# Eight token lists broadcast over the partitions by DMA, and a shorter chain to the quantised table, at the start of a fused language-model tower

## The reference

```python
def fake_quant(w):
    scale = max(abs(w)) / 127
    return round(w / scale) * scale
e = fake_quant(emb_weight)[x]                 # x: (8, 512) token numbers below 125
e = pad(e, one step ahead)                    # context of two tokens
h = relu(e[t-1] * w[0] + e[t] * w[1])         # w = fake_quant(conv_weight), per channel
h = h + attn(layernorm(h))                    # a linear recurrence over the 512 steps
h = h + ffn(layernorm(h))                     # 8 experts by position: 128 -> 512 -> 128, gelu
```

## Time and profile before

| | before |
|---|---|
| device time, median of 3 (lowest to highest) | 210.72 us (210.22 to 210.72) |
| span of the profiled execution (its own time outside the span is not on the page) | 206.2 us |
| TensorE busy | 181.0 us (88%) |
| VectorE busy | 143.2 us (69%) |
| ScalarE busy | 116.5 us (56%) |
| GpSimd busy | 97.5 us (47%) |
| moved by DMA | 7.60 MB |

### The profile page before, as it was taken

The page is one execution under the profiler, slowest core; times in us unless marked ns, Lnnn a source line. Parts: engine busy times, 40 slices in busy tenths (PEclk is TensorE's granted clock), DMA queues, the critical chain, the costliest instruction groups (busy, mean ns, idle before and its releaser), DMA issues. The chain is left out here.

```text
span 206.2 us, 4072 instructions
## 1 busy us (share of the span) xinstructions
PE 181.0 (88%) x1407; PEld 163.3 (79%) x1407; DVE 143.2 (69%) x411; ACT 116.5 (56%) x317; POOL 97.5 (47%) x144
## 2 busy tenths in 40 slices
PE   0498999999999999999694999988979979996993
PEld 0276789999899987887594898987969969995891
DVE  1859956753444434669587685995977959569994
ACT  2037986554433355454444577847759577693771
POOL 0116644999200002239576184672843917656441
PEclk9999999999999999999999699999999999999999
DMA  5991000000000000000000000010100100010012
GB/s 137 399 423 62 3 0 5 2 0 3 0 0 3 0 0 2 3 0 0 0 3 2 0 3 0 0 51 5 51 0 3 52 0 27 27 51 2 3 52 102
DMA packets 2566, 7.60 MB, mean 37 GB/s; under 512 B 309, under 2 KB 1122, under 8 KB 2290
## 3 DMA queue, kind: packets, MB, share of 16 engines
q1 hardware_dynamic: 2258, 7.15, 9.1%
q10 hardware_dynamic: 288, 0.20, 0.4%
HBM read 5.25 MB, written 2.10 MB: 36 GB/s over the span
## 5 line engine op out<-in xcount | busy, mean ns | idle before, releaser
L421 POOL TENSOR_TENSOR hid_p<-hid_f,hid_p 128x256 fp32r<-128x256 f32 x56 | 40.2, 734 | 35.8 <-ACT hid_p L566 27.6
L564 ACT ACTIVATE hid_f<-bank,pa 128x256 f32<-128x256 f32 x64 | 30.3, 478 | 22.6 <-PE bank L1091 22.6
L1091 PE MATMUL bank<-xaT_p,fc_p 128*128 128x256 f32 x192 | 35.7, 297 | 0.8 <-ACT hid_f L564 0.7
L1111 PE MATMUL bank<-hid_p,out_hi 128*128 128x256 f32 x128 | 33.6, 288 | 0.6 <-POOL hid_p L421 0.5
L473 ACT ACTIVATE X<-bank 128x128 f32<-128x128 f32 x64 | 17.6, 279 | 23.3 <-PE bank L935 23.1
L1091 PEld LDWEIGHTS bank<-xaT_p,fc_p 128*128 128x128 f32 x192 | 27.3, 191 | 3.4 <-issue 2.0
L932 PE MATMUL bank<-uT,pa 128*128 128x128 f32 x128 | 25.1, 280 | 0.1
L843 DVE TENSOR_SCALAR xp<-h,mv,rstd 128x128 f32<-128x128 f32 x32 | 22.5, 762 | 3.3 <-POOL rstd L439 3.3
L1111 PEld LDWEIGHTS bank<-hid_p,out_hi 128*128 128x128 f32 x128 | 23.8, 188 | 1.2 <-POOL hid_p L421 0.9
L935 PE MATMUL bank<-X,pa 128*128 128x128 f32 x120 | 23.2, 275 | 0.0
L566 ACT ACTIVATE hid_p<-bank,pa 128x256 fp32r<-128x256 f32 x48 | 23.0, 478 | 0.0
(11 more groups left out here) (123 smaller groups left out, 384.4 us busy)
## 6 DMA issues: line engine op xcount, KB each, us to landing
fc_w<-in_fc SPq DMA_DIRECT2D x2, 2048.0 KB, 11.2
out<-res SPq DMA_DIRECT2D x7, 256.0 KB, 2.0
pb<-in_pack_b SPq DMA_DIRECT2D x1, 320.0 KB, 4.2
pa<-in_pack_a SPq DMA_DIRECT2D x1, 279.0 KB, 3.5
out<-res SPq DMA_DIRECT2D x2, 128.0 KB, 1.7
conv_w<-in_conv ACTq DMA_DIRECT2D x1, 128.0 KB, 3.4
pc<-in_pack_c ACTq DMA_DIRECT2D x1, 66.5 KB, 3.8
rowsel<-in_rows SPq DMA_DIRECT2D x1, 64.0 KB, 3.8
```

Of the source, the lines that this page charges most:

```text
L421: nc.gpsimd.tensor_tensor(hid_p[1][:, half, c, :], hid_f[:, m % HID_SLOTS, :], hid_p[0][:, half, c, :].bitcast(F32), ALU.subtract).then_in ...
L564: full = nc.scalar.activation(hid_f[:, m % HID_SLOTS, :], src, ACT.Gelu, bias=bias)
L1091: last = mm(bank[5 + n % 2][:, 0:HALF], fc1_p[w][:, e * HID + c * P:e * HID + (c + 1) * P], xaT_p[m][:, b % 2, half, :], start=(k == 0), s ...
L1111: last = mm(out_bank(b, half)[:, half * HALF:(half + 1) * HALF], out_p[w][:, e, c * CH:(c + 1) * CH], hid_p[m][:, half, c, :], start=(c == ...
```

## The change

The 16 rows of ids, the cast, the selecting matrix and the spreading matmuls go. Each sequence's 544 ids are loaded as int32 onto 125 partitions, by one transfer that reads the same row 125 times: the first between `emb_w` and `pa`, the other seven after `pw` and ahead of `pb`. They count on three semaphores: batch 0, batches 1 to 3, batches 4 to 7. `one_hot(b)` is one instruction, reads SBUF, clips from above and compares; it is placed one round ahead of its gather where it was two.

The row maxima are transposed from a view that repeats them over 128 columns, so that the maximum is taken on all partitions at once. The rounding constant is added in the pass that scales and taken off in the passes that multiply by the taps; the bf16 product is computed anew in place of a cast. VectorE quantises the convolution weights before it reads the transposed maxima.

Gathers alternate between bank 2 and bank 0, and the first six `transpose_u` between bank 3 and bank 1. The waits of `gather`, `transpose_u` and the first `fuse_piece` follow from that. (Left out below: names of tensors and semaphores that only follow.)

```diff
 
             fc2_w = sb_early("fc2_w", [P, NE * HID])
             fc1_w = sb_early("fc1_w", [P, NE * HID])
-            ids_i = sb_early("ids_i", [2 * NB, EXT * NCH // 2], I32)
-            ids_b = sb_early("ids_b", [2 * NB, EXT * NCH // 2], BF16)
-            rowsel = sb_early("rowsel", [2 * NB, 2 * NB, P], BF16)
+            ids_i = sb_early("ids_i", [VOC, NB, EXT * NCH], I32)
...
@@ -320,6 +318,17 @@
         def scan_work(j, n):
             return plan[8 * (j + 3) + n]
 
+        IDS_GROUPS = (1, 3, 4)
+
+        def ids_group(b):
+            return 0 if b == 0 else 1 if b < 4 else 2
+
+        def gather_bank(b):
+            return bank[(2, 0)[b % 2]]
+
+        def u_t_bank(b):
+            return bank[1 if b % 2 == 1 and b < 6 else 3]
+
         P2_BANKS = ((4, 5, 0, 1), (6, 7))
 
         def fuse_bank(e):
@@ -351,10 +360,11 @@
             @block.sync
             def _(sp):
                 sp.dma_start(emb_w[:], emb).then_inc(ld_emb, 16)
-                sp.dma_start(ids_i[:], ids).then_inc(ld_ids, 16)
-                sp.dma_start(rowsel[:].rearrange("r j p -> r (j p)"), rows).then_inc(ld_ids, 16)
+                sp.dma_start(ids_i[:, 0, :], ids[0:1, :].broadcast_to([VOC, EXT * NCH])).then_inc(ld_ids[0], 16)
                 sp.dma_start(pa[:], pack_a).then_inc(ld_pa, 16)
                 sp.dma_start(pw[:, 1, :], pack_a[:, PA["a"]]).then_inc(ld_pa, 16)
+                for b in range(1, NB):
+                    sp.dma_start(ids_i[:, b, :], ids[b:b + 1, :].broadcast_to([VOC, EXT * NCH])).then_inc(ld_ids[ids_group(b)], 16)
                 sp.dma_start(pb[:], pack_b).then_inc(ld_pb, 16)
...
@@ -482,12 +492,12 @@
                         act.wait_ge(gat_done, b + 1)
                         if b == 0:
                             act.wait_ge(tab_ready, 1)
-                        nc.scalar.activation(h[:, b, :], bank[2][:], ACT.Relu, scale=scale_h[:]).then_inc(h_ready, 1)
+                        nc.scalar.activation(h[:, b, :], gather_bank(b)[:], ACT.Relu, scale=scale_h[:]).then_inc(h_ready, 1)
                     for t in prep_tasks(b, 0):
                         copy_out_prep(t)
                     if b >= 2:
                         act.wait_ge(u_t_done, b - 1)
-                        nc.scalar.activation(uT[:, b - 2, :, :].rearrange("p i k -> p (i k)"), bank[3][:],
+                        nc.scalar.activation(uT[:, b - 2, :, :].rearrange("p i k -> p (i k)"), u_t_bank(b - 2)[:],
...
@@ -612,38 +622,34 @@
                 dve.wait_ge(ld_conv, 16)
                 chained(nc.vector.tensor_reduce(scale_c[:], conv_w[:], AX.X, ALU.max, apply_absolute_value=True))
                 nc.vector.tensor_scalar(scale_c[:], scale_c[:], 1.0 / QMAX, None, ALU.mult).then_inc(scale_c_ready, 1)
-                dve.wait_ge(amax_t_done, 1)
-                nc.vector.tensor_reduce(amax_row[:], bank[6][0:1, 0:VOC], AX.X, ALU.max).then_inc(amax_row_ready, 1)
                 dve.wait_ge(scale_c_ready, 1)
                 chained(nc.vector.reciprocal(inv_c[:], scale_c[:]))
-                chained(nc.vector.tensor_scalar(q_c[:], conv_w[:], inv_c[:], None, ALU.mult))
-                nc.vector.tensor_scalar(q_c[:], q_c[:], ROUND, -ROUND, ALU.add, ALU.add).then_inc(q_c_ready, 1)
-
-                dve.wait_ge(ld_ids, 32)
-                nc.vector.tensor_scalar(ids_b[:], ids_i[:], -1.0, float(VOC - 1), ALU.max, ALU.min).then_inc(ids_ready, 1)
-                dve.wait_ge(amax_bc_done, 1)
-                chained(nc.vector.tensor_scalar(scale_e[:], bank[7][:, 0:1], 1.0 / QMAX, None, ALU.mult))
+                chained(nc.vector.tensor_scalar(q_c[:], conv_w[:], inv_c[:], ROUND, ALU.mult, ALU.add))
+                nc.vector.tensor_scalar(q_c[:], q_c[:], -ROUND, None, ALU.add).then_inc(q_c_ready, 1)
+
+                dve.wait_ge(amax_t_done, 1)
+                chained(nc.vector.tensor_reduce(amax_all[:], bank[6][:, 0:VOC], AX.X, ALU.max))
+                chained(nc.vector.tensor_scalar(scale_e[:], amax_all[:], 1.0 / QMAX, None, ALU.mult))
                 chained(nc.vector.reciprocal(inv_e[:], scale_e[:]))
-                chained(nc.vector.tensor_scalar(q_e[:], emb_w[:], inv_e[0:VOC, :], None, ALU.mult))
-                chained(nc.vector.tensor_scalar(q_e[:], q_e[:], ROUND, -ROUND, ALU.add, ALU.add))
+                chained(nc.vector.tensor_scalar(rounded[:], emb_w[:], inv_e[0:VOC, :], ROUND, ALU.mult, ALU.add))
                 dve.wait_ge(q_c_ready, 1)
 
-                for tap in range(2):
-                    last = nc.vector.tensor_tensor(prod[:, tap, :], q_e[:], q_c[0:VOC, tap * CH:(tap + 1) * CH], ALU.mult)
-                chained(last)
-                chained(nc.vector.tensor_copy(tab[:, 0], prod[:]))
+                both = rounded[:].unsqueeze(1).broadcast_to([VOC, 2, CH])
+                q_taps = q_c[0:VOC, :].rearrange("p (t c) -> p t c", t=2)
+                nc.vector.scalar_tensor_tensor(out=prod[:], in0=both, scalar=-ROUND, in1=q_taps,
+                                               op0=ALU.add, op1=ALU.mult)
+                chained(nc.vector.scalar_tensor_tensor(out=tab[:, 0], in0=both, scalar=-ROUND, in1=q_taps,
+                                                       op0=ALU.add, op1=ALU.mult))
                 nc.vector.tensor_tensor(scale_h[:], scale_e[:], scale_c[:], ALU.mult)
                 nc.vector.tensor_tensor(tab[:, 1], prod[:], tab[:, 0], ALU.subtract).then_inc(tab_ready, 1)
 
                 def one_hot(b):
-                    for s in range(2):
-                        n = 2 * b + s
-                        dve.wait_ge(idb_done, n + 1)
-                        if b >= 2:
-                            dve.wait_ge(gat_done, b - 1)
-                        w = EXT * NCH // 2
-                        nc.vector.tensor_scalar(onehot[:, b % 2, s * w:(s + 1) * w], bank[n % 2][0:VOC, 0:w],
-                                                pc[0:VOC, PC["iota"]], None, ALU.is_equal).then_inc(oh_ready, 1)
+                    group = ids_group(b)
+                    dve.wait_ge(ld_ids[group], 16 * IDS_GROUPS[group])
+                    if b >= 2:
+                        dve.wait_ge(gat_done, b - 1)
+                    nc.vector.tensor_scalar(onehot[:, b % 2, :], ids_i[:, b, :], float(VOC - 1),
+                                            pc[0:VOC, PC["iota"]], ALU.min, ALU.is_equal).then_inc(oh_ready, 1)
...
                 dve.wait_ge(ld_pc, 16)
                 one_hot(0)
-                one_hot(1)
                 for b in range(NB + 1):
-                    if b + 2 < NB:
-                        one_hot(b + 2)
+                    if b + 1 < NB:
+                        one_hot(b + 1)
...
@@ -875,7 +880,8 @@
                         if e == 0:
                             pe.wait_ge(ld_fc2, 16)
                             pe.wait_ge(ld_pb, 16)
-                            pe.wait_ge(oh_ready, 2 * NB)
+                            pe.wait_ge(h_ready, NB)
+                            pe.wait_ge(uT_ready, 6)
...
@@ -890,34 +896,28 @@
                     for c in range(HC):
                         fuse_piece(e, c)
 
-                def spread_ids(b):
-                    for s in range(2):
-                        n = 2 * b + s
-                        if n >= 2:
-                            pe.wait_ge(oh_ready, n - 1)
-                        mm(bank[n % 2][:, 0:EXT * NCH // 2], rowsel[:, n, :], ids_b[:], start=True,
-                           stop=True).then_inc(idb_done, 1)
-
                 def gather(b):
-                    pe.wait_ge(oh_ready, 2 * b + 2)
-                    if b >= 1:
-                        pe.wait_ge(h_ready, b)
+                    pe.wait_ge(oh_ready, b + 1)
+                    if b >= 2:
+                        pe.wait_ge(h_ready, b - 1)
                     for q in range(NQ):
                         for n, (tap, part) in enumerate([(0, 0), (0, 1), (1, 0), (1, 1)]):
 
                             at = (q * TQ + tap) * NCH
-                            last = mm(bank[2][:, q * CH:(q + 1) * CH], onehot[:, b % 2, at:at + P], tab[:, part, tap, :],
+                            last = mm(gather_bank(b)[:, q * CH:(q + 1) * CH], onehot[:, b % 2, at:at + P], tab[:, part, tap, :],
                                       start=(n == 0), stop=(n == 3))
                     last.then_inc(gat_done, 1)
 
                 def transpose_u(b):
                     pe.wait_ge(u_ready, b + 1)
                     pe.wait_ge(u_act_ready, sum(n < NQ for n in U_DVE[:b + 1]))
-                    if b >= 1:
+                    if b >= 6:
                         pe.wait_ge(uT_ready, b)
+                    elif b >= 2:
+                        pe.wait_ge(uT_ready, b - 1)
                     for q in range(NQ):
                         s = slice(q * CH, (q + 1) * CH)
-                        last = nc.tensor.transpose(bank[3][:, s], u[:, b % 2, s], ident)
+                        last = nc.tensor.transpose(u_t_bank(b)[:, s], u[:, b % 2, s], ident)
```

(35 more changed lines are left out.)

## The result

The changed kernel took 218.33 us in the median of 4 runs (216.77 to 218.62), the kernel before 210.47 beside it (208.18 to 210.72): a ratio of 1.042, 95% interval 1.036 to 1.048. (A kernel has a faster and a slower state on this chip; the ratio compares runs in the faster one alone and is not the quotient of the two medians, 1.037.) It is slower by 7.9 us by the medians and 8.9 by the ratio, where 2.2 were forecast, and the time lies outside the stated range, 211.0 to 214.5. The direction was as forecast, and so was its cause, loads on few engines. Two further losses on top of it, in the last ids loads and in TensorE's clock, were not in the sum.

What follows compares the result with a forecast made beforehand. The prediction took TensorE, full from 32 us on, as the bound, so delays entering that part move the end. Ids loads on five engines outweigh the earlier start: 210.7 + 2.2 = 212.9 us, range 211.0 to 214.5.

Steps and rivals of the forecast that it cites:

- Part 1, the chain: Start, chain to the quantised table: table at 7.91 us against 8.84, first gather at 8.5 instead of 10.05, 1.55 us earlier.
- Part 2: Rounds: the matmuls that spread the ids go, 0.3 to 0.4 us a round; VectorE saves 0.4 a round.
- Part 3: Second banks for gathers and `transpose_u`: help only when the next one-hot is there; the new fused-piece wait costs nothing.
- Part 4, five engines: Eight ids broadcast loads: 125 rows use five engines, 2.25 us each; TensorE's full part starts 2.2 us later; chance 0.70.
- The missing landing time: List of transfers: `emb_w`, the one load over 125 rows, has no landing time, taken as supporting five engines.
- Group 1: Ids loads of batches 1 to 3, sharing one semaphore: landing forecast at 14.2 us (13.3 to 15.0).
- Loads 4 to 7 follow: 14.2 + 9.0 = 23.2: Last ids group lands at 23.2 us, where `one_hot(4)` waits; gather 4 starts at 23.75 instead of 20.92.
- upper bound, 24.3: Latest landing forecast for ids loads 4 to 7, giving a delay of 3.3 us.
- the slow TensorE: Rival: after idling, gathers 2 to 5 and prep matmuls stay slow, up to 0.8 us a round; 214.5 us; chance 0.08.
- the likeliest case: Five engines carry each ids load, delaying TensorE's full part by 2.2 us: 212.9 us (211.2 to 214.0), chance 0.70.
- 4.5 us around the span: Time outside the 206.2 us span, up to the median of 210.72, taken as unchanged.
- hidden loads: Rival: sixteen engines share each ids load, 0.73 us each, no one-hot waits; 207.9 us; chance 0.12.

Runs made afterwards that it cites:

- E9: The changed kernel with ids loads over 128 rows, SP also waiting for `emb_w` before issuing anything else; 208.48 us, ratio 0.997 to the kernel before.
- E8: 128-row kernel, first ids load after `pa` and `pw`, three ids loads for eight, `pc` issued ahead of `conv_w`; 208.29 us, ratio 0.993 to the kernel before.
- E7: The kernel before with only the new chain to the table, ids still by matmuls; 209.07 us, ratio 0.998 to the kernel before.
- E12: E9 with batch 1's ids on a semaphore of their own (four groups: 1, 1, 2, 4); 205.94 us, ratio 0.985 to the kernel before.
- E1: The changed kernel with each ids load over 128 rows instead of 125; 207.88 us, ratio 0.995 to the kernel before.
- E2: The changed kernel, still 125 rows, SP issuing `pb`, `sel` and fc loads only after the last ids group landed; 211.66 us, ratio 1.014.
- E3: The changed kernel with 20 identity matmuls filling TensorE's idle stretch ahead of gather 4; 216.93 us, ratio 1.039 to the kernel before.
- E11: The changed kernel with 20 filling matmuls ahead of gather 4, on the same chip as E10; 215.93 us, ratio 1.033 to the kernel before.
- E4: E1 with all gathers in bank 2, transposes of `u` in bank 3 and the earlier waits; 207.50 us, ratio 0.994 to the kernel before.
- E6: The changed kernel with each ids load over 126 rows instead of 125; 208.25 us, ratio 0.995 to the kernel before.
- E10: The changed kernel once more, unaltered, on the chip of E11; 218.32 us, ratio 1.045 to the kernel before.

## Why the prediction was wrong

**Part 1, the chain: right in its own length, wrong in its start.** From the transpose to the start of the gather the prediction has 8.5 - 4.94 = 3.6 us. In the changed kernel that stretch is 7.15 to 10.58, 3.4 us; in E9, 4.27 to 8.44, 4.2, with the wait for `pw`. But the prediction left `pc` at 4.94. It landed at 6.4 to 7.8 in all nine profiles that have a load of 266 to 279 KB issued next to it; in E8, which has `pc` first, `conv_w` was late instead. In the four with small loads next to it, or none (before, E7, E9, E12), it was there at 4.2 to 5.2. The first gather started at 10.58. In the changed kernel this cost nothing, for `one_hot(1)` waited until 14.76 anyway; E12 takes it away from E1's kernel and splits the groups besides, and starts gather 7 at 29.16 instead of 30.97.

**Part 2: a little more than forecast, and covered. Part 3: nothing, as forecast.** The sum gave the matmuls that go 0.65 us between gather 4 and the full part. Where the clock stayed up (E2, E3, E11), gather 4 to gather 7 take 10.4 us instead of 11.2 before: 0.8. What of it is the matmuls' and what the shorter one-hot's, no run separates. In the changed kernel the fall of the clock covers it (12.05 us). For the second banks E4 shows that they bring nothing, in the kernel of 128 rows. The one-hot took 0.50 us in one pass, the value taken.

**Part 4, five engines: right.** 129 GB/s at a share of 0.33, and the 10 us between 125 and 128 rows, with 126 on the fast side, show it. The missing landing time, which the prediction read as a sign of five, goes with 14 engines too (E6). The Trainium skill ("DMA: Bandwidth & Descriptors", section "Why a DMA increments its semaphore by 16 and not by 1") has the rule; by that rule 126 rows go over 14 engines and 125 over 5. The share of 0.33 with 125 rows and the speed of E6 agree with it, though no run counts the 14. Group 1 landed at 14.76, 14.2 forecast.

**The step that failed: "Loads 4 to 7 follow: 14.2 + 9.0 = 23.2".** It assumed that the ids loads keep their rate with `pb` and the fc loads issued behind them. SP was busy with the seven ids loads until 12.5 us and then issued `pb` and the fc loads, which ran beside the last ids loads instead of behind them; together they moved 270 GB/s at a share of 1.02, and the group landed at 27.59. That is 4.4 us over the forecast, 3.8 of them given back by E2's wait. The prediction's upper bound, 24.3, came from rows between 5.0 and 14.7 us, in which no load over 125 rows was in flight (`emb_w` had landed at 3.92), and could not show this.

**The second: the slow TensorE as a rival of its own with 0.08.** It was priced at up to 1.6 us on top of the likeliest case, and that price was about right: 1.6 us in the changed kernel's profile, 1.9 between E10 and E11. What was wrong is that it stood beside the likeliest case and not in it. It was also argued from gathers that were slow with the clock column at 1.00, while here the column fell to 0.50 in an idle stretch of 4.6 us; the prediction had this stretch at 2.4 us (21.3 to 23.7).

At the start of gather 7 the terms add up: 2.2 forecast + 4.4 for the landing + 1.6 for the clock - 0.15 for what part 2 gave more = 8.05, against 40.20 - 32.13 = 8.07.

**A smaller one: 4.5 us around the span.** Every execution whose span is on record is 1.8 to 1.9 us longer than its span, so the span of 206.2 belongs to one of about 208.1 us and not to one of 210.72; runs of the kernel before lie between 207.9 and 212.9. The forecast difference of 2.2 does not rest on it, but the base of 210.7 is a high one: the same forecast on 208.1 would have been 210.3.

**Of the rivals**, hidden loads is what E1 builds, and the equal times (207.9 and 207.88) are luck. The rival had it 2.8 us below the kernel before; E1 is 0.5%, 1.1 us, below it on its own chip. Its first gather came 1.4 us later than the rival had it.

**Open:** why loads over 5 or 14 engines and the loads beside them move less together (252 to 279 GB/s at full share against over 400); by what a big load beside `pc` delays it; and why the first gathers take 1.86 to 1.89 us with the clock column at 1.00, in the kernel before and in the changed one alike, so that this duration alone is no sign of a fallen clock.

## What to carry to other kernels

Look at the number of rows of a transfer before its bytes: 125, 126 and 128 rows behaved here as if the largest divisor up to 16 set the number of engines, and three unused rows (128 for 125) were worth 10 us. When you price a transfer, price what is issued after it too, and what a longer wait does to TensorE's clock. And when a wait goes, look for the next one in line: E9 gained 1.5 us at the first gather and lost it at a semaphore shared by three loads; only with that split (E12) did the change pay. The split without E9's wait was not run; `one_hot(1)` waits 0.41 us in E1, so little is to be had there.

## What was not expected of the hardware

- Ids loads over 125 rows and fc loads in flight together moved 270 GB/s at a DMA share of 1.0; apart from each other they ran at 128 GB/s (share 0.33) and 408 (share 1.04).
- The granted clock fell to 0.50 while TensorE idled between 23.6 and 28.15 us, and stayed there while it worked again, until about 32. That cost 1.6 to 1.9 us, and 20 matmuls in the idle stretch saved it.
- A load of 266 to 279 KB on SP's queue, issued within 0.4 us of a 66 KB load on ACT's, moved the landing of the latter from 4.2 to 5.2 us to between 6.4 and 7.8.
